# Last layer's experts: first group chosen ahead of the later norms, later pairs turned and routed behind the first units

## The reference, cut to what matters

```python
def _L3_ffn_ref(x, Wg, bg, Wi, Wo, A, B):     # x: (16, 128, 256), layer-normed
    logits = einsum('bsd,ed->bse', x, Wg) + bg          # 4 experts
    scores = softmax(logits)
    topv, topi = top_k(scores, 2)
    w = sum(one_hot(topi) * topv[..., None], axis=-2)
    base = einsum('bsd,fd->bsf', x, Wi)                 # 1024 hidden
    lora_low = einsum('bsd,erd->bser', x, A)            # rank 4
    lora = einsum('bser,efr->bsef', lora_low, B)
    h = relu(base[:, :, None, :] + lora)
    out = einsum('bse,bsef,df->bsd', w, h, Wo)
x = x + tanh(g_ffn[3]) * out
```

## Time and profile before

| what | value |
|---|---|
| three runs | 1596.36, 1606.6, 1609.18 us; median 1606.6 |
| profiled execution, its own time | 1601.59 us |
| its span in the trace | 1599.7 us, 28308 instructions |
| mean granted clock of TensorE | 0.902 of full |
| TensorE products busy | 1338.5 us, 84% of the span |
| VectorE, ScalarE, GpSimd busy | 1137.4, 910.0 and 715.0 us (71%, 57%, 45%) |
| last layer's experts (1443.7 to the end) | 156 us, mean granted clock 0.88 |

### The profile page before, as it was taken

The page is one execution under the profiler, slowest core; times in us unless marked ns, Lnnn a source line. Parts: engine busy times, 40 slices in busy tenths (PEclk is TensorE's granted clock), DMA queues, the critical chain, the costliest instruction groups (busy, mean ns, idle before and its releaser), DMA issues. The chain is left out here.

```text
span 1599.7 us, 28308 instructions
## 1 busy us (share of the span) xinstructions
PE 1338.5 (84%) x9642; PEld 1115.8 (70%) x9642; DVE 1137.4 (71%) x2475; ACT 910.0 (57%) x1954; POOL 715.0 (45%) x753
## 2 busy tenths in 40 slices
PE   3699977899999999879984579999878965656898
PEld 1445555799999999745664579999776852345787
DVE  7447755588888989558966648888565658785654
ACT  3236652577777877556742337778526457464432
POOL 2223200376776776604320128888502940454444
PEclk7699997899999999988996689999999989676999
DMA  5000003456666666230012217667511000101000
GB/s 186 1 1 1 1 11 102 181 216 259 234 253 240 241 263 233 103 110 1 2 53 93 79 45 247 234 241 260 192 43 62 1 1 1 33 1 62 1 27 27
DMA packets 60828, 173.69 MB, mean 109 GB/s; under 512 B 10304, under 2 KB 42048, under 8 KB 51088
## 3 DMA queue, kind: packets, MB, share of 16 engines
q1 hardware_dynamic: 53200, 151.42, 26.5%
q0 software_dynamic: 7488, 20.46, 3.7%
HBM read 155.34 MB, written 16.52 MB: 107 GB/s over the span
## 5 line engine op out<-in xcount | busy, mean ns | idle before, releaser
L1846 POOL TENSOR_TENSOR l0m_e_DL<-l0m_e_DN,l0m_e_DH 128x256 fp32r<-128x256 f32 x192 | 174.2, 917 | 98.2 <-ACT l0m_e_DH L1689 96.6
L1754 DVE TENSOR_TENSOR l0m_e_UL<-l0m_e_U,l0m_e_UH 128x512 fp32r<-128x512 f32 x192 | 168.7, 884 | 12.6 <-ACT l0m_e_UH L1679 12.1
L1615 PE MATMUL PS<-l0m_e_CH,l0m_e_UH 128*128 128x256 f32 x480 | 138.4, 288 | 2.0 <-DVE l0m_e_CL L1789 2.0
L1615 PE MATMUL PS<-l0m_e_CH,l0m_e_UL 128*128 128x256 f32 x480 | 136.5, 284 | 0.0
L1615 PE MATMUL PS<-l0m_e_CL,l0m_e_UH 128*128 128x256 f32 x480 | 136.4, 284 | 0.0
L1679 ACT CAST l0m_e_UH<-l0m_e_U 128x512 fp32r<-128x512 f32 x192 | 117.9, 615 | 0.0
L1846 POOL TENSOR_TENSOR l1m_e_DL<-l1m_e_DN,l1m_e_DH 128x256 fp32r<-128x256 f32 x96 | 87.8, 930 | 17.7 <-ACT l1m_e_DH L1689 16.8
L1615 PEld LDWEIGHTS PS<-l0m_e_CH,l0m_e_UH 128*128 128x128 f32 x480 | 92.7, 193 | 2.2 <-ACT l0m_e_UH L1679 2.2
L1648 PE MATMUL PS<-l0m_e_DH,l0m_e_HH 128*128 128x256 f32 x312 | 88.6, 284 | 5.0 <-issue 2.6
L1615 PEld LDWEIGHTS PS<-l0m_e_CL,l0m_e_UH 128*128 128x128 f32 x480 | 92.8, 193 | 0.0
L1615 PEld LDWEIGHTS PS<-l0m_e_CH,l0m_e_UL 128*128 128x128 f32 x480 | 92.7, 193 | 0.0
(11 more groups left out here) (618 smaller groups left out, 4779.2 us busy)
## 6 DMA issues: line engine op xcount, KB each, us to landing
l0m_e_U<-in_l_up SPq DMA_DIRECT2D x24, 2048.0 KB
l0m_e_DN<-in_l_down SPq DMA_DIRECT2D x24, 1024.0 KB, 4.9
l1m_e_U<-in_l_up SPq DMA_DIRECT2D x24, 1024.0 KB, 6.3
l1m_e_DN<-in_l_down SPq DMA_DIRECT2D x24, 512.0 KB, 3.9
l1a_GA<-results_by_choice SPq DMA_DIRECT2D x16, 256.0 KB, 5.9
l1m_c_GA<-results_by_choice SPq DMA_DIRECT2D x16, 256.0 KB, 5.0
Z<-in_l_b_rows SPq DMA_DIRECT2D x24, 128.0 KB, 3.0
X<-in_x SPq DMA_DIRECT2D x4, 512.0 KB, 8.4
```

What stands on the lines that cost most here:

```text
L1615: ins = nc.tensor.matmul(hb(u)[:, a * SLOTS:(a + 1) * SLOTS], w[:, f % RING, k, a, :], x[:, t % 2, k, :], start=(p == 0), stop=(p == len(p ...
L1754: nc.vector.tensor_tensor(UL[:, f % RING, :, :, :], U[:, t % 2, :, :, f * P:(f + 1) * P], UH[:, f % RING, :, :, :].bitcast(F32), ALU.subtr ...
L1846: nc.gpsimd.tensor_tensor(DL[:, f % RING, :], DN[:, t % 2, f, :], DH[:, f % RING, :].bitcast(F32), ALU.subtract).then_inc(s_dl, 1)
```

## The change

Six things move in `l3_ffn`; no product and no element of work is dropped, apart from the three fifths of a memset of zeros over which `parts` writes anyway.

1. VectorE does columns(0) and the routing of group 0 ahead of the norms of sequences 8 to 15, which now stand behind the remainder in BMS. ScalarE likewise norms sequences 9 to 15 (odd) only behind copy_piece(2).
2. Pairs 4 and 5 are turned behind first(0), pairs 6 and 7 behind first(1); logits of sequences 8 to 11 follow first(1), of 12 to 15 first(2), one unit later than before.
3. The cast of WI and its remainder are cut in four parts, and the exponential of group 0 and CH stand ahead of the cast. The cast of WO and its remainder are cut in four, one part behind each of ScalarE's read(0) to read(3).
4. The memset of LO shrinks to the two strips between its written parts, and comes after the second group's factors.
5. The exponential of group 1 moves from u = 2 to u = 3.
6. The diagonals 1, 2 and 3 move from behind adds 3, 6 and 8 to behind adds 5, 7 and 9.

```diff
--- before.py
+++ after.py
@@ -3300,9 +3300,13 @@
                        PS[:, 7, 0:(B - FIRST) * NG3].rearrange("p (b n) -> p b n", n=NG3))
                 group = (slice(0, FIRST), slice(FIRST, B))
                 rows_bank = lambda n, r: PS[:, 4 + 2 * (n % 2) + r // 2, (r % 2) * D:(r % 2 + 1) * D]
+                wi_part = lambda q: slice(q * FF // 2, (q + 1) * FF // 2)
+                wo_part = lambda q: slice(2 * q, 2 * q + 2)
                 piece_bank = lambda q: q if q < 3 else 6 + q % 2
                 PIECES = 3 * NBK
                 first_piece = {6: (3, 5), 7: (5, 6), 9: (6, 8), 10: (8, 10), 11: (10, 12)}
+                late_turn = {0: (4, 5), 1: (6, 7)}
+                late_logits = {1: FIRST + 4, 2: FIRST + 8}
                 SPLIT = FIRST + 4
 
                 with nc.Block() as block:
@@ -3387,7 +3391,7 @@
                             pe.wait_ge(s_hh, u + 1)
                             pe.wait_ge(s_hl, u + 1)
                             if u == 0:
-                                pe.wait_ge(s_wl, 2)
+                                pe.wait_ge(s_wl, 8)
                             if f == 0 and n == 1:
                                 pe.wait_ge(s_cp, PIECES)
                             if f == 0 and n >= 2:
@@ -3404,20 +3408,22 @@
                         turn(0)
                         turn(1)
                         logits(0, 0, FIRST)
-                        for i in range(2, pairs):
+                        for i in range(2, 4):
                             turn(i)
                         logits(1, FIRST, SPLIT)
-                        pe.wait_ge(s_one, 3)
+                        pe.wait_ge(s_one, 4)
                         for q in range(3):
                             piece(q)
                         pe.wait_ge(s_bh, 1)
                         pe.wait_ge(s_bl, 1)
-                        pe.wait_ge(s_wl, 1)
+                        pe.wait_ge(s_wl, 4)
                         for u in range(N + 6):
                             if u < N:
                                 first(u)
-                            if u < 2:
-                                logits(1, SPLIT + u * 4, SPLIT + u * 4 + 4)
+                            for i in late_turn.get(u, ()):
+                                turn(i)
+                            if u in late_logits:
+                                logits(1, late_logits[u], late_logits[u] + 4)
                             if 2 <= u < N + 2:
                                 second(u - 2)
                             if u in first_piece:
@@ -3477,27 +3483,34 @@
                         deviation(2, FIRST, B)
                         normalise(1)
                         normalise(3)
+                        normalise(5)
+                        normalise(7)
                         columns(1)
-                        for i in range(2, pairs):
-                            normalise(2 * i + 1)
-                        act.wait_ge(s_wi, 16)
-                        nc.scalar.copy(WIH[:, :, :], WI[:, :, :]).then_inc(s_wh, 1)
-                        columns(3)
                         exponential(0)
                         cols_high(0)
-                        columns(5)
-                        columns(7)
+                        act.wait_ge(s_wi, 16)
+                        for q in range(2):
+                            for k in range(KD):
+                                nc.scalar.copy(WIH[:, k, wi_part(q)], WI[:, k, wi_part(q)]).then_inc(s_wh, 1)
+                        columns(3)
                         act.wait_ge(s_ld, 48)
                         nc.scalar.copy(BMS[:, :], BM[:, :]).then_inc(s_bh, 1)
-                        act.wait_ge(s_wo, 16)
-                        nc.scalar.copy(WOH[:, :, :], WO[:, :, :]).then_inc(s_wh, 1)
                         for q in range(2):
                             copy_piece(q)
                         copy_piece(2)
+                        for i in range(4, pairs):
+                            normalise(2 * i + 1)
                         for u in range(N + 3):
                             if u < N:
                                 read(u)
-                            if u == 2:
+                            if u == 0:
+                                act.wait_ge(s_wo, 16)
+                            if u < 4:
+                                nc.scalar.copy(WOH[:, wo_part(u), :], WO[:, wo_part(u), :]).then_inc(s_wh, 1)
+                            for i in late_turn.get(u, ()):
+                                if i % 2:
+                                    columns(i)
+                            if u == 3:
                                 exponential(1)
                             if u == 3:
                                 cols_high(1)
@@ -3523,22 +3536,28 @@
                                 ALU.mult).then_inc(s_dg, 1)
 
                         nc.gpsimd.memset(SC[:, :, :], -1.0).then_inc(s_one, 1)
-                        nc.gpsimd.memset(LO[:, :, :, :], 0.0).then_inc(s_one, 1)
                         nc.gpsimd.memset(ONES[:, :], 1.0).then_inc(s_one, 1)
-                        for n, (lo, raw, high) in enumerate(((WIL, WI, WIH), (WOL, WO, WOH))):
-                            pool.wait_ge(s_wh, n + 1)
-                            nc.gpsimd.tensor_tensor(lo[:, :, :], raw[:, :, :], high[:, :, :].bitcast(F32),
-                                                    ALU.subtract).then_inc(s_wl, 1)
-                            if n == 0:
-                                diagonal(0)
+                        pool.wait_ge(s_ok, 2)
+                        for at in (E4 * RK, 32 + E4 * RK):
+                            nc.gpsimd.memset(LO[:, :, :, at:at + E4 * RK], 0.0).then_inc(s_one, 1)
+                        for q in range(2):
+                            for k in range(KD):
+                                pool.wait_ge(s_wh, 2 * q + k + 1)
+                                nc.gpsimd.tensor_tensor(WIL[:, k, wi_part(q)], WI[:, k, wi_part(q)],
+                                                        WIH[:, k, wi_part(q)].bitcast(F32), ALU.subtract).then_inc(s_wl, 1)
+                        diagonal(0)
+                        for q in range(4):
+                            pool.wait_ge(s_wh, 5 + q)
+                            nc.gpsimd.tensor_tensor(WOL[:, wo_part(q), :], WO[:, wo_part(q), :],
+                                                    WOH[:, wo_part(q), :].bitcast(F32), ALU.subtract).then_inc(s_wl, 1)
                         for u in range(N):
                             pool.wait_ge(s_h1, u + 1)
                             pool.wait_ge(s_h2, u + 1)
                             if u >= HELD:
                                 pool.wait_ge(s_hl, u - HELD + 1)
                             nc.gpsimd.tensor_tensor(HR(u), HA(u), HB(u), ALU.add).then_inc(s_h, 1)
-                            if u in (3, 6, 8):
-                                diagonal({3: 1, 6: 2, 8: 3}[u])
+                            if u in (5, 7, 9):
+                                diagonal({5: 1, 7: 2, 9: 3}[u])
 
                     @block.vector
                     def _(dve):
@@ -3610,7 +3629,6 @@
                             ch.step(nc.vector.tensor_copy(LR[:, :, v, :], LW[:, :, v, :]))
                             ch.step(nc.vector.reciprocal(RT[:, 0, v], M8[:, v, 0]))
                             ch.wait()
-                            dve.wait_ge(s_one, 2)
                             for at in (0, 64):
                                 ch.step(nc.vector.tensor_copy(LO[:, :, v, at:at + E4 * RK], LR[:, :, v, :].bitcast(F32)))
                             nc.vector.tensor_tensor(LO[:, :, v, 32:32 + E4 * RK], LW[:, :, v, :], LR[:, :, v, :].bitcast(F32),
@@ -3657,26 +3675,27 @@
                         normalise(0)
                         normalise(2)
                         row_factors(dve, ch, s_sd, 2, s_ok, FIRST, B)
-                        columns(0)
                         for i in range(2, 4):
                             normalise(2 * i)
+                        columns(0)
                         shifted(0)
-                        for i in range(4, pairs):
-                            normalise(2 * i)
                         columns(2)
                         softmax(0)
-                        columns(4)
                         order(0)
-                        columns(6)
                         choose(0)
                         parts(0)
                         cols_low(0)
                         dve.wait_ge(s_bh, 1)
                         nc.vector.tensor_tensor(BMS[64:RS, :], BM[64:RS, :], BMS[64:RS, :].bitcast(F32),
                                                 ALU.subtract).then_inc(s_bl, 1)
+                        for i in range(4, pairs):
+                            normalise(2 * i)
                         for u in range(N + 4):
                             if 2 <= u < N + 2:
                                 read(u - 2)
+                            for i in late_turn.get(u, ()):
```

(2 more changed lines are left out.)

## The result

The changed kernel is slower by half a per cent: 1608.15 us in the median of 20 runs against 1599.62 us in the 20 runs of before, a ratio of 1.0052 with a 95% interval of 1.0037 to 1.0067, which is 6 to 11 us. The profiled execution has a span of 1608.7 us against 1599.7. Everything up to the last layer was 0.8 us shorter in it, so I count the last layer from VectorE's first instruction in it (1443.77 us before, 1443.01 after) to the end of the span: 155.9 us before, 165.7 us after, 9.8 us more.

A forecast was written before the change was run, and what follows sets the result against it. TensorE, dense from 1502 us behind a 58 us head, was taken to bound the last layer; -0.8 + 3.7 + 4.3 + 4.3 = +11.5 us on 1603.4 gave 1614.9 us, range 1603 to 1623.

The forecast's parts named there:

- head, up to the second group's LO: Last layer's start until the second expert choice: reordered work makes it 0.8 us shorter, bounds -3.5 to +1.9.
- stall ahead of piece 5: TensorE behind unit 5's second product: waits through VectorE's read, GpSimd's add 5 and diagonal 1, +3.7 us.
- stall ahead of piece 11: TensorE behind piece 10: waits for diagonal 3, itself behind add 9 and VectorE's CL subtraction, +4.3 us.
- low clock behind them: TensorE after the two stalls: a slow-clock stretch costs 2.15 us each, 4.3 us together, bounds 0 and 5.
- Diagonal 2 was hidden: GpSimd's diagonal 2 behind add 7 ends at 1511.3, before piece 8 at 1511.78: no stall, 0.5 us to spare.
- the skill's variant of 3.3 us: At piece 11: shared port lets the diagonal in directly behind its add, so the stall is 3.3 us, sum 1.0 less.
- rival B: Both stalls occur but TensorE's clock holds through one or both: sum +7.2 to +9.4 us, chance 0.20.
- I take two at each: Four turns between units 0 and 2: two at the low clock, two at the full one, 2.8 us together.
- The lower bound I gave for unit 0 to 2: Units 0 to 2 on TensorE: all at full clock without waits leaves 2.5 us of the 4.3 us earlier start.
- C: Head becomes longer, +1.9 us, through GpSimd's late adds and low-clock turns, with slower recovery: +14 to +16 us, chance 0.14.
- D: Second choice sheds VectorE's waits for GpSimd, about 4.2 us; if the clock holds, 0.5 to 2 us faster; chance 0.05.
- E: Only one of TensorE's two stalls shows, the other's GpSimd work running in an earlier hole: +5 to +6 us, chance 0.09.

## Why the prediction was right, and where it was off

The direction and the mechanism were right; the expected +11.5 us of span became +9.0, and the 1614.9 us became 1608.15. By steps, in the terms of the sum (us, from the starts of TensorE's pieces and units in both traces):

| term | predicted | measured |
|---|---|---|
| head, up to the second group's LO | -0.8 | -2.5 |
| stall ahead of piece 5 | +3.7 | +3.75 |
| stall ahead of piece 11 | +4.3 | +4.31 |
| low clock behind them | +4.3 | +1.7 and +2.5 |
| layer | +11.5 | +9.8 |

TensorE's instructions ahead of the two pieces, before (second(5) and piece 10):

```profile
1500.03 0.39 PE L3381 MATMUL PS<-l3f_LT,l3f_BMS 80*128 80x512 f32 x1
...
1516.36 0.60 PE L3354 MATMUL PS<-CONST,l3f_LO 128*80 128x128 f32 x4
```

and piece 10 after:

```profile
1518.45 0.60 PE L3358 MATMUL PS<-CONST,l3f_LO 128*80 128x128 f32 x4
```

(The first stall: second(5) to piece 5 was 1500.26 - 1500.03 = 0.23 us and is 1500.66 - 1496.68 = 3.98. The second: piece 10 to piece 11 was 0.43 us and is 1523.19 - 1518.45 = 4.74. The clock: piece 5 to unit 8 and its second product 1.7 longer, piece 11 to unit 12's second product 2.5 longer. The rest of the 9.8 is -0.1.)

**The diagonals.** Both waits, their releasers and lengths came as read from the order of the loops and the durations in the earlier trace rows. Diagonal 2 was hidden, as said. Diagonal 3 waited behind CL, as the alternation had it, so the skill's variant of 3.3 us didn't occur.

**The clock.** Its sum came out right, 4.2 us for 4.3. The rival B, that the clock holds, fell in this trace and in that of the kernel before with late diagonals, and the run that kept TensorE busy shows the term by itself. The argument for it was weaker than it looked, though: I took from the 2.1 us gap before that such a gap ends at the low clock. The gap at the same place was 1.96 us after the change, and the products behind it ran at 1.00 (the second row of the stretches); of the twelve traces of this case only four show the low clock there. And with diagonal 1 alone back, the clock held through the whole gap of 4.13 us and fell only later, at a cost of 1.6 us. So that 2.15 us for each came so near in the sum is in part luck. The gaps of 3.6 us and more, in the changed kernel and in the one before with late diagonals, were all followed by low clock.

**The head** was mis-sized, by 1.7 us. Unit 0's conditions came almost as worked out: VectorE finished the BMS remainder at 1465.67, which is 1466.4 on the clock of before, where I had 1466.9. What failed is the step "I take two at each": all four turns ran at the full clock, 0.80 us for two of them (1468.40 to 1469.20) instead of a mean of 1.4, and 0.87 us for the other two, together 1.1 us less, and unit 0 took 2.6 us instead of the 3.1 that I charged. With the 0.5 at the start that is about the 1.9 us by which VectorE's first read came ahead of my 1480.1. VectorE's first read came at 1477.42, 2.4 us earlier on the layer's clock, and the second choice took 13.8 us instead of 13.9, where I had charged 0.3 us less. It won 0.9 us at its first steps and 0.4 us at the scores, and lost most of it to two waits that I hadn't charged, 0.59 us for second(1) and 0.36 us for the exponential; 0.1 us was left. The lower bound I gave for unit 0 to 2 (2.5 us left) is what happened.

**The other rivals.** C (longer head) fell: GpSimd's add 0 stood behind the fourth WOL part until 1481.50, but add 0 wasn't what VectorE waited for; the scores lost 0.5 us to that part, not 1.1. D fell, since VectorE still stood behind adds in one-hots (1.43 us) and rounding (1.32 us). E fell: both stalls showed, and the second comes without the first too.

**The level.** Of the 6.8 us between forecast and median, 3.8 are the base: I put the sum on 1603.4, the mean of four executions, and 20 runs gave 1599.6. The chance of 0.81 for "within 1%" was the right call.

## What to carry to other kernels

When work in one queue moves behind an item of a loop, look up in the other queues' loops what that item waits for, and compare with the place of the one who needs the moved work: here a wait for add 5 stood directly behind the product that add 5 itself needs, and that is a stall of the whole round trip (read, add, diagonal: 3.75 us). Move producer and consumer together, or put the consumer of a late result where its own reader is just in time: one unit later for pieces 3 to 5 gained 2.5 us, in one table, where the change's whole new head gained 2.5 to 3.4. And charge a gap on TensorE together with the low clock behind it: here 0.4 to 0.6 of the gap's length again, differing between executions.

## What the runs showed of the hardware

The same head takes different times, with the clock: in three executions of the old head, VectorE's first read came 36.8, 38.2 and 38.2 us behind the layer's first instruction, and in those with the changed head between 33.4 and 34.8 us. Unit 0 took 2.06 us in the first of the old heads, mostly at the full clock, and 3.7 us in the other two, at the low one. A gap of about 2 us ahead of unit 6 ended at the low clock in four executions (2.08 us before; 1.96, 1.97 and 1.96 us in the runs with only diagonal 1 back, with the whole memset first and with CL earlier) and at the full one in the other eight (1.96 us changed, 2.11 us in the one before with late diagonals). Rows of TensorE with only diagonal 1 back, and before with late diagonals:

```profile
1484.49 0.80 PE L3376 MATMUL PS<-l3f_CH,l3f_WIH 128*128 128x512 f32 x1 [1.96 <-DVE Z L3653]
```

```profile
1484.23 0.50 PE L3372 MATMUL PS<-l3f_CH,l3f_WIH 128*128 128x512 f32 x1 [2.11 <-DVE Z L3635]
```

The products behind it started every 0.43 us in the first and every 0.23 us in the second. The changed kernel's gap was 1.96 us as well and ended at the full clock, so the length of the gap doesn't decide it. And a difference of 1.4 us in one trace is not yet an effect of the code.
The Trainium skill ("TensorE: Matmul & The Clock Gate", section "What's actually happening") says that the observation which sets the clock runs free of the kernel, so that the moment of switching varies between runs; the three readings of one head agree with it.

The alternation of VectorE and GpSimd is no rule without exception. In the changed kernel VectorE did two instructions one behind the other while GpSimd's add 4 stood waiting:

```profile
1492.55 0.68 DVE L3660 TENSOR_TENSOR l3f_HL<-Z,l3f_HH 128x512 fp32r<-128x512 f32 x1
1493.14 1.22 DVE L3643 TENSOR_TENSOR l3f_CL<-ZT,l3f_CH 128x1024 fp32r<-128x1024 f32 x1
```

```profile
1492.76 2.74 POOL L3558 TENSOR_TENSOR Z<-l3f_WI,Z 128x512 f32<-128x512 f32 x1 [3.04 <-DVE Z L3653]
```

An add takes 1.28 us alone, so this one waited 1.46 us, until the end of both (1494.36). Before, the add in this place came between the two: there the first of VectorE's two had itself waited, for the diagonal. What decides between the two cases is not shown.
